# Row maxima of a pair: the last small operations on GpSimd, maxima chained through a starting value, the transposition one item later

## The reference

```python
scores = q @ k.T / sqrt(16)                     # "plain"
gsa_scores = scores + position_sensitivity * splat_attn   # "guided"
std_out = out_proj(softmax(where(mask, scores, neg)))
gsa_out = out_proj(softmax(where(mask, gsa_scores, neg)))
attn = (1 - blend) * std_out + blend * gsa_out
x = layernorm(x + attn); x = layernorm(x + ffn(x))   # gated, 2 of 4 hidden values kept
```

## Time and profile before

| | us |
|---|---|
| timed runs (3) | 395.86, 396.21, 396.52; median 396.21 |
| profiled execution, span from first to last instruction (it comes with no other time) | 396.0 |
| PE busy | 372.8 (94%) |
| DVE busy | 303.9 (77%) |
| ACT busy | 229.6 (58%) |
| POOL busy | 125.7 (32%) |
| chain of work that ended last, by engine | PE 69%, DVE 19%, ACT 6%, the rest 6% |

### The profile page before, as it was taken

The page is one execution under the profiler, slowest core; times in us unless marked ns, Lnnn a source line. Parts: engine busy times, 40 slices in busy tenths (PEclk is TensorE's granted clock), DMA queues, the critical chain, the costliest instruction groups (busy, mean ns, idle before and its releaser), DMA issues.

```text
span 396.0 us, 6714 instructions
## 1 busy us (share of the span) xinstructions
PE 372.8 (94%) x2234; PEld 255.1 (64%) x2234; DVE 303.9 (77%) x900; ACT 229.6 (58%) x451; POOL 125.7 (32%) x173
## 2 busy tenths in 40 slices
PE   6998999999999999999999999999889899999995
PEld 6666568565665665675664664764435488888884
DVE  2766999997897897897898898795024367999955
ACT  3965443675675685684784774775766836443100
POOL 8377657403303303302302312284395200000000
PEclk9998999999999999999999999999989999999999
DMA  6062540450540540540550558000000000000003
GB/s 201 22 105 47 81 81 4 67 95 10 88 70 4 87 75 6 89 73 4 82 82 3 80 86 319 4 2 0 5 0 2 0 2 0 0 2 0 2 0 106
DMA packets 12907, 19.70 MB, mean 50 GB/s; under 512 B 5492, under 2 KB 8564, under 8 KB 12872
## 3 DMA queue, kind: packets, MB, share of 16 engines
q1 hardware_dynamic: 10328, 18.18, 22.9%
q0 software_dynamic: 1536, 1.07, 1.6%
q10 hardware_dynamic: 1008, 0.02, 0.1%
HBM read 5.26 MB, written 1.05 MB: 16 GB/s over the span
## 4 chain that ended last, share of the span: by engine, by line
PE 69%; DVE 19%; ACT 6%; issue 2%; DMA 2%; SPq 1%; POOL 0%; DVEq 0%; ACTq 0%
PE ps L937 17%; PE ps L963 14%; PE ps L902 13%; DVE ps L1270 11%; PE ps L863 7%; PE ps L765 5%; PE ps L767 5%; PE ps L766 5%; DVE mpart L1263 2%; PE ps L924 2%; ACT pr L713 2%; DMA x_sb<-_attn_hidden_states_dram 2%; DVE mpart L1270 2%; PE ps L847 1%; PE ps L827 1%
## 5 line engine op out<-in xcount | busy, mean ns | idle before, releaser
L713 ACT ACTIVATE pr<-ps 128x512 f32<-128x512 f32 (+2 forms) x320 | 154.8, 571 | 75.8 <-PE ps L963 74.7
L1270 DVE CUSTOM_DVE_ANT_0 ps<-ps,causal 128x512 f32<-128x512 f32 (+3 forms) x256 | 144.9, 615 | 19.0 <-PE ps L902 18.2
L902 PE MATMUL ps<-k_st,q_st 65*128 65x512 f32 (+5 forms) x384 | 120.9, 369 | 3.5 <-DVE mpart L1270 2.8
L963 PE MATMUL ps<-q_st,k_st 67*128 67x512 f32 (+7 forms) x384 | 122.2, 363 | 0.3 <-ACT pr L713 0.3
L963 PEld LDWEIGHTS ps<-q_st,k_st 67*128 67x128 f32 (+1 forms) x384 | 68.3, 191 | 39.4 <-issue 21.5
L902 PEld LDWEIGHTS ps<-k_st,q_st 115*128 115x128 f32 (+1 forms) x384 | 67.9, 190 | 25.8 <-DVE mpart L1270 15.7
L937 PE MATMUL ps<-pr,vx 128*32 128x512 f32 (+3 forms) x768 | 74.1, 497 | 1.9 <-ACT o_sb L699 1.0
L558 POOL TENSOR_SCALAR_AFFINE_SELECT pr<-pr 128x512 f32<-128x512 f32 x64 | 40.5, 634 | 87.7 <-ACT pr L713 87.3
L1263 DVE TENSOR_REDUCE mpart<-ps 128x1 f32<-128x384 f32 (+2 forms) x96 | 54.9, 596 | 7.3 <-PE ps L902 7.0
L937 PEld LDWEIGHTS ps<-pr,vx 128*32 128x32 f32 x768 | 19.4, 109 | 32.1 <-issue 17.4
L1270 DVE DVE_READ_ACCUMULATOR2_ANT mpart<- 128x1 f32 x256 | 36.0, 141 | 0.0
(11 more groups left out here) (190 smaller groups left out, 497.5 us busy)
## 6 DMA issues: line engine op xcount, KB each, us to landing
q_st<-base_hiq SPq DMA_DIRECT2D x28, 64.0 KB
k_st<-base_hik SPq DMA_DIRECT2D x28, 64.0 KB
q_st<-feat_hiq SPq DMA_DIRECT2D x28, 64.0 KB
k_st<-feat_hik SPq DMA_DIRECT2D x28, 64.0 KB
x_sb<-_attn_hidden_states_dram SPq DMA_DIRECT2D x4, 256.0 KB, 6.5
raw<-in_L_ffn_w_gate_dram SPq DMA_DIRECT2D x1, 1024.0 KB, 4.8
raw<-in_L_ffn_w_up_dram SPq DMA_DIRECT2D x1, 1024.0 KB, 7.0
wd<-in_L_ffn_w_down_dram SPq DMA_DIRECT2D x1, 1024.0 KB, 9.1
```

What stands on the lines that cost most here:

```text
L713: act.activation(pr[:, s % NP, 2 * hh + vs[0]:2 * hh + vs[-1] + 1, d:BANK], src, ACT.Exp, scale=SCALE).then_inc(exp_done, 1)
L902: mm = pe.matmul(ps[:, slot, at:at + n], q_st[b][0:rows, hh, i * P:(i + 1) * P], k_st[b][0:rows, hh, first:first + n], start=(v == v0), st ...
L963: mm = pe.matmul(ps[:, bank, j * width:(j + 1) * width], k_st[b][0:rows, hh, kt * P:(kt + 1) * P], q_st[b][0:rows, hh, q:q + width], start ...
L1270: ins = dve.tensor_tensor_reduce(out=ps[:, slot, at:at + n], in0=ps[:, slot, at:at + n], in1=causal[:, BANK - n:BANK], scale=1.0, scalar=- ...
```

## The change

- `mpart` loses its index of the piece: it holds first pieces only. The new `mfull` has two buffers, by the pair's parity, and receives the full maxima.
- The masked `tensor_tensor_reduce` of a last piece takes the first piece's maximum as its starting value (a `[128, 1]` operand in SBUF) in place of -3e38. It waits until that first piece is done. Four rows of pair 0 (plain, tiles 4 and 5, two heads) can't, as their last piece comes first; VectorE joins them by one small maximum at `rows 0`.
- The other four small operations of "rows" move from VectorE to GpSimd, into `rows(p)`, which waits until the pair's last maximum is done. The rounding is a `tensor_scalar` (x 1, + 0) instead of a copy. In a step GpSimd does `rows`, then the mask, then the DMAs.
- From pair 2 on VectorE waits before each maximum until the `rows` of two pairs before are ready (the buffer of the same parity).
- `TURN_LAG` is 5: `turn_max` of the pairs 1 to 6 moves back by one item within step 9. For pairs 0 and 7 its place is the same.

```diff
-    TURN_LAG = 4
+    TURN_LAG = 5
+    last_max = [max(r for r, it in enumerate(ring) if it[:2] == ("max", p)) for p in range(PAIRS)]
-        mpart = sb("mpart", [P, PIECES, T, KC, 2], F32)
+        mpart = sb("mpart", [P, T, KC, 2], F32)
+        mfull = sb("mfull", [P, 2, T, KC, 2], F32)
 GpSimd:
+            def rows(p):
+
+                pool.wait_ge(ring_free, last_max[p] + 1)
+                if p == 0:
+                    pool.wait_ge(joined, 1)
+                plain = mfull[:, p % 2, :, :, 0].rearrange("p t h -> p h t")
+                guided = mfull[:, p % 2, :, :, 1].rearrange("p t h -> p h t")
+                pool.tensor_scalar(mdiff[:, 0], plain, -1.0, None, ALU.mult).then_inc(row_half, 1)
+                pool.tensor_tensor(mdiff[:, 1], plain, guided, ALU.subtract).then_inc(row_half, 1)
+                pool.wait_ge(row_half, 3 * p + 2)
+                if p >= 1:
+                    pool.wait_ge(ring_full, ring_at[("turn_max", p - 1)] + 1)
+                pool.tensor_scalar(mrow[:, :, 0].bitcast(F32R), mdiff[:], 1.0, 0.0, ALU.mult, ALU.add).then_inc(row_half, 1)
+                pool.wait_ge(row_half, 3 * p + 3)
+                pool.tensor_tensor(mrow[:, :, 1].bitcast(F32R), mdiff[:], mrow[:, :, 0], ALU.subtract).then_inc(rows_ready, 1)
...
+            rows(0)
             maxima(0)
             constant_rows(2)
             for s in range(len(steps)):
+                for it in at_step[s]:
+                    if it[0] == "rows":
+                        rows(it[1])
                 mask(s)
 VectorE:
                 if it[0] == "rows":
-
-                    dve.wait_ge(ring_free, r)
-                    for c in range(1, PIECES):
-                        t = min(i for i in range(T) if len(row_pieces(i)) > c)
-                        link(dve.tensor_tensor(mpart[:, 0, t:T], mpart[:, 0, t:T], mpart[:, c, t:T], ALU.max))
-                    plain = mpart[:, 0, :, :, 0].rearrange("p t h -> p h t")
-                    guided = mpart[:, 0, :, :, 1].rearrange("p t h -> p h t")
-                    dve.tensor_scalar(mdiff[:, 0], plain, -1.0, None, ALU.mult)
-                    link(dve.tensor_tensor(mdiff[:, 1], plain, guided, ALU.subtract))
-                    if it[1] >= 1:
-                        dve.wait_ge(ring_full, ring_at[("turn_max", it[1] - 1)] + 1)
-                    link(dve.tensor_copy(mrow[:, :, 0].bitcast(F32R), mdiff[:]))
-                    dve.tensor_tensor(mrow[:, :, 1].bitcast(F32R), mdiff[:], mrow[:, :, 0], ALU.subtract).then_inc(rows_ready, 1)
+                    if it[1] == 0:
+
+                        dve.wait_ge(ring_free, r)
+                        tiles = slice(TPG, TPG + HALF // P)
+                        dve.tensor_tensor(mfull[:, 0, tiles, :, 0], mfull[:, 0, tiles, :, 0], mpart[:, tiles, :, 0],
+                                          ALU.max).then_inc(joined, 1)
                     continue
...
+                    if p >= 2:
+                        dve.wait_ge(rows_ready, p - 1)
                     if c < len(row_pieces(i)) - 1:
-                        dve.tensor_reduce(mpart[:, c, i, hh, v:v + nv],
+                        dve.tensor_reduce(mpart[:, i, hh, v:v + nv],
...
+                        chained = c > 0 and ring_at[it] > first_piece(it)
+                        if chained:
+                            dve.wait_ge(ring_free, first_piece(it) + 1)
...
-                                scale=1.0, scalar=-3e38, op0=ALU.add, op1=ALU.max,
-                                accum_out=mpart[:, c, i, hh, v + j:v + j + 1])
+                                scale=1.0, scalar=mpart[:, i, hh, v + j:v + j + 1] if chained else -3e38,
+                                op0=ALU.add, op1=ALU.max, accum_out=mfull[:, p % 2, i, hh, v + j:v + j + 1])
```

More of the change, by code:

```diff
@@ L321, in build_kernel @@
         ring_full, ring_free = sem("ring_full"), sem("ring_free")
-        rows_ready = sem("rows_ready")
+        rows_ready, row_half, joined = sem("rows_ready"), sem("row_half"), sem("joined")
         s_full, exp_done = sem("s_full"), sem("exp_done")
@@ L1225, in normalize, with first_piece @@
                                       ALU.subtract, ALU.mult).then_inc(done, 1)
+            def first_piece(it):
+                _, p, hh, i, _, v, nv = it
+                return max(ring_at[x] for x in ring if x[:5] == ("max", p, hh, i, 0) and x[5] <= v < x[5] + x[6])
             dve.wait_ge(consts, 7)
```

## The result

The changed kernel is slower. On one chip its median was 400.65 us (398.96 to 403.06, 4 runs) against 396.07 for the kernel before (4 runs): ratio 1.0125, 95% interval 1.0083 to 1.0168. Measured again on another chip it was 402.3 us against 396.22, ratio 1.0152 (1.0111 to 1.0193). The prediction was 392.0 us, 390.3 to 395.4; its sign was wrong.

A forecast was written before the change was run, and what follows sets the result against it. The prediction took PE to set the time, and DVE where PE waits for it. Its terms, 6.1 - 0.1 - 0.9 - 0.24 - 0.1 - 0.5 = 4.2 us, took 396.2 to 392.0 us, range 390.3 to 395.4.

The forecast's parts named there:

- The small operations leave DVE: At the ends of pairs 1 to 6, DVE starts the next pair's items 1.02 us earlier: 6.1 us gained.
- GpSimd's chain: The four small operations on GpSimd after a pair's last maximum take 1.04 us, hidden up to 1.37.
- rival B: GpSimd is too slow and PE stands waiting at the transposition; 399 us, chance 9%.
- Rival C: At pairs' ends PE, freed from DVE, meets the exponentials' gate at once; no net gain, 396.2 us, chance 8%.
- The wait of a last piece for its first: On DVE, 0.12 us where the first piece is just before; in later pairs 0.02 a pair, 0.1 in all.
- The opening: In pair 0, twelve waits and GpSimd's chain delay PE's transposition: -0.9 us, then -0.24 from two more waits.
- The operand: The [128, 1] starting value in SBUF, read by 124 maxima, costs 0.01 us each where DVE bounds: -0.5 us.
- rival A: The starting-value operand costs 0.06 us per maximum on DVE, 3.2 us and 0.8 more; 395.4 us, chance 13%.
- Pair 7: In the last pair the transposition waits for the small operations, slower on GpSimd by some 0.1: -0.1 us.
- Rival D: Chained maxima and GpSimd's operations block each other, 4.2 us lost over seven pairs; 396.2 us, chance 4%.

The follow-up runs named there:

- e5: The changed kernel with the last pieces' waits kept but a constant -3e38 as starting value, first pieces left out of the maxima; 397.9 us, ratio 1.0029.
- e4: The changed kernel with chained maxima reading a constant -3e38 column and no wait for first pieces, which are left out; 393.59 us, ratio 0.9941.
- e8: The changed kernel with only the order of maxima changed, so no last piece comes right behind its first; 392.89 us, ratio 0.9901.
- e1: The changed kernel without the chained starting value, VectorE joining the pieces in every pair, rows still on GpSimd; 391.93 us, ratio 0.9907.

## Why the prediction was wrong

- **The small operations leave DVE: right.** From values to values across a pair's end it was 6.63 and is 5.72 us; 0.91 where 1.02 was forecast. Six of them: 5.5 us gained instead of 6.1.
- **GpSimd's chain: right.** 1.08 against 1.04 us, hidden in the pairs 1 to 6, so rival B is out. Rival C (a stall that is hidden anyway) is out by the same 0.91.
- **The wait of a last piece for its first: this step failed.** The prediction said 0.12 us, made of a start 0.04 after the end of a 16-column predecessor; behind a reduction of PSUM it is 0.14 after its end (57.78 to 57.92), and with the 0.09 of overlap that is lost, 0.23. That size was wrong by a factor of two, and so was the place: "three of them with idle time behind", 0.02 a pair, where e5 shows 0.33. Two of the four waits lie in b, ahead of the values of step 7; they cost 0.26 and 0.23, and the idle time that should have taken them was a single gap of 0.23. (The prediction's "1.4 us better" for a wait that costs nothing takes the opening's twelve waits in full, 12 x 0.12; in its own sum the waits make at most 0.9 + 0.24 + 0.1 = 1.24.)
- **The opening: failed by the same step.** 2.66 us instead of 0.9, and up to the first values 0.73 instead of 0.24. Of the 2.66 e5 gives 1.96 to the waits.
- **The operand: failed, and rival A had it nearly right.** Start to start it costs 0.07 behind a first piece (0.61 to 0.68) and 0.02 behind another maximum (0.65 to 0.67). The two rows that it was chosen from, operations with tensors in SBUF, did not tell. From e4's and e5's stretches it is 0.7 in the opening when DVE is late already (18.48 - 17.78), 0.25 to the first values, and 0.35 a pair (b 0.25, a 0.1): 3.4 us over seven pairs and the opening, where the prediction said 0.5 and rival A 3.2 (and 0.8 for idle time used up). Rival A's total, 395.4, was still 5 us too low, as it kept the prediction's price for the wait.
- **Pair 7:** 0.25 instead of 0.1 (PE waited 0.78 for GpSimd at 278.40).
- **Rival D** (DVE and GpSimd block each other) is not seen: chained maxima take 0.75 to 0.76 with and without GpSimd beside them, and e8 carries the operand at no such cost.
- **Not foreseen:** the spell at the lower clock, 2.3 us in one profile and 3.7 in the other; 0.35 us outside the span; and 0.68 us in the FFN, which the change does not touch. Its 192 matmuls on `yt` take 48.56 us from the first start to the last in the profile of before and 49.24 after, at a granted clock of 1.00 in both; the eleven experiments' profiles have 49.13 to 49.25. All of these kernels have the new `mfull`; whether that is the reason was not tried, and there is only one profile of before.

The sum with the measured terms, without the spell: 5.5 (pairs' ends) - 2.7 (opening) - 0.7 (to the first values) - 4.5 (a and b: 0.52 in pair 0, 3.97 over pairs 1 to 6) - 0.25 (pair 7) - 0.7 (FFN) - 0.35 (outside the span) = -3.7 us. The changed kernel's two runs at a granted clock of 0.989 took 398.96 and 399.8 us; the kernel before takes 395.6 to 397.3 at 0.990 to 0.991, with a median of 396.0. That is 3.0 and 3.8 slower at nearly the same clock. The rest of the 4.6 in the medians (400.65 - 396.07) goes with the clock: its other two runs had 0.981.

The two profiled spans differ by 5.0 us. The changed kernel reaches the opening's second 384-column first piece 1.8 earlier; it loses 4.0 in the opening (of which 1.3 in a spell at the lower clock at 44 to 48 us), 2.3 up to the first values, nothing from there to the values of pair 7, where the gain at the pairs' ends makes up for a, b and the rest of the spell, and 0.55 behind them.

The mistake in the reading, more than in any size: DVE was judged by its mean, 26.32 of 30.45 us, and by the one gap next to a wait. The edit puts something on 124 maxima, and b is a stretch in which PE waits for DVE. The prediction counted five instructions a pair there and did not add what waits and operands do to each other, once the last idle gap of the stretch is used up: 0.33 and 0.16 alone, 0.58 together.

## What to carry to other kernels

A VectorE instruction's wait for the one just before it was a real cost here wherever VectorE was the bound: it gives up the overlap and adds a gap, 0.23 us together. Put one independent instruction in between; the same chain with another order was 8 us faster here, the spell at the lower clock included. Before moving work off an engine, separate the parts: moving the small operations was worth 4 us (e1), and the chain, which saves a join of 0.2 us a pair, cost 8.7 (400.65 - 391.93).

## What the runs showed of the hardware

- A VectorE maximum that waits for the 512-column reduction right before it starts 0.14 us after that one's end, 0.83 from start to start, against 0.60 without a wait. Between operations of 16 columns the gap was 0.04. With one or more instructions in between the wait is free (e8). Why the gap is 0.14 here and 0.04 there stays open.
- A [128, 1] starting value in SBUF makes a masked maximum of 512 columns take 0.755 us in the mean of 124, against 0.714 for 160 with a constant (e5).
- GpSimd does an operation on 16 or 32 columns in 0.21 to 0.27 us and starts 0.10 to 0.17 after the VectorE instruction that it waits for.
- The join on VectorE took 0.17 us with GpSimd idle and 0.52 to 0.67 where a 512-column GpSimd operation was running when it started; in each of these profiles it ended 0.02 to 0.04 after that operation.
- TensorE's clock fell to the lower level for some 7 to 10 us in three of five profiles of kernels whose last pieces wait for the instruction right before them in the opening, and in none of the eight others at that place. What sets it off is open.
